# Half of the residual row joins each expert row of a routed attention layer; the last head and the first expert tiles overlap

## The chip, the cores and the metric

The kernel runs on one core of a Trainium2 chip. The metric is the device time of one execution in microseconds (us): a median of 1658.82 us over 3 runs, from 1657.81 to 1659.13.

The engines are PE (TensorE, matrix products), DVE (VectorE), ACT (ScalarE), POOL (GpSimd) and SP (SyncE, which here only starts DMA transfers). Each runs its own instruction stream; the streams meet at semaphores that one side raises and the other waits for. 16 DMA engines move data between the chip's memory (HBM) and the on-chip buffers. PE writes its sums to PSUM, eight banks of 128x512 fp32.

## The reference, cut to what matters

```
x : (2, 2048, 512) fp32;  xn = layernorm(x)
attention: 16 heads of width 32 with a latent width of 128, causal softmax
           o = concat(heads) @ Wo.T + bo
experts:   logits = xn @ gate_w + gate_b; the two best of 8 experts per token
           ffn = mean over the two of relu(xn @ expert_w[e] + expert_b[e])
result = x + o + ffn
```

There are 4096 tokens, or 32 tiles of 128. Each token has two expert rows, so 8192 expert rows are computed. They are sorted by expert and padded to PT = 72 tiles of 128 rows, so that each tile belongs to one expert.

## The kernel before

**Stages.** The first stage (to about 265 us) normalizes the rows, makes queries, keys and values, writes all of them to HBM, and works out for each token and choice its place in the sorted order (`place`) and, turned round, the token of each place (`ids`). The second stage runs 32 heads (batch x head), with PE as its busiest engine. The third computes the 72 expert tiles. The fourth projects the 32 token tiles of attention output and adds everything up.

**The head stage and its last head.** A head is NU = 20 units; each is two blocks of scores (L1274), their exponentials on ACT (L821) and, two units later, the product with the values (L1296). Units on the diagonal of the causal mask need a mask from POOL (L609) before that product; of the last chunk these are units 17 and 18 of 20. When a head's values are summed, its result goes a long way, issued by SP and spread over the next head's units: `ot_moves` (L441) copies the sums and denominators out, SP loads the denominators (L481), DVE inverts them (`invert`, L1062), SP stores them and loads them spread over the partitions (L487, L495), POOL adds two halves (`add_halves`, L612), DVE multiplies (`scale`, L1070), ACT and POOL split the product into two fp16 parts (L815, `low_part` L619), and SP keeps it in `attnT` (L502). For the last head there is no next one to spread this over. POOL also splits the expert weights into two fp16 parts during the heads (`split`, L625), one 128x512 piece per head, through the buffer `stage`, which is the memory of `x_g0`.

**The expert stage.** For tile n, POOL copies one column of `ids` to `cur_id` (L679), waits for its own copy, and gathers 128 rows of the normalized input (2 KB each, L682) into one of four buffers `x_g`; it may run four tiles ahead of PE's transposes (`gt_ps`). PE transposes tile n+1 (`turn`, L1321) and then runs the 12 matmuls of tile n (`experts`, L1339); ACT copies the transposed tile to SBUF as fp16 (L840). DVE makes the result in two operations: scale and expert bias (L1104), then relu and output bias (L1108) into one of two buffers `y_sb`. SP stores it (L530). Ahead of the loop PE waits for the last head's values to have been copied out (L1312); POOL has gone through its instructions of the last head before it gathers. SP has kept the last head (L502), loaded the projection's weights `rest` (1 MB, L524) and the residual rows of eight token tiles (`residual`, L513) before its first store.

**The last stage.** POOL waits for all stores of the expert rows (L691), then issues two gathers of 128 rows of 2 KB for each of 32 token tiles (L697), eight tiles ahead of DVE. PE makes 12 matmuls per tile (`project`, L1361) into eight PSUM banks. DVE adds in three operations (`sums`): L1118 takes the bank and the residual tile `xc` and sets the bank free (`dveE`), L1120 and L1121 add the two gathered rows. SP stores the tile (L520) and loads the residual of the tile eight further on (L514).

**Memory.** `arena2` is used by the head stage (`probs`, `q_st`, `k_st`, `v_sb`) and again by the expert stage (`xg_T`, `y_sb`, `x_ahead`, `xc`). Four `probs` buffers take its first 4096 columns, `q_st` the next 2048.

**Order.** There is no planner. The lags of the heads' steps are written out as constants in units (`ADD_LAG`, `LO_LAG`, `KEEP_LAG` and others, L315), and each engine's `heads` walks the units in one order. Loops are `Fori`; what stands in one is written once.

## Time and profile before

| what | value |
|---|---|
| median of 3 runs | 1658.82 us |
| the profiled execution itself | 1658.73 us |
| its span, first to last instruction | 1657.0 us |
| PE busy | 1516.7 us, 92% |
| DVE busy | 1149.0 us, 69% |
| ACT busy | 901.7 us, 54% |
| POOL busy | 580.0 us, 35% |
| mean granted clock of PE | 0.969 of full |

The profile is one execution. "Busy" is the time in which an engine works on an instruction; matmuls overlap one another, so PE's busy time isn't PE at its peak. In a timeline each row has a start in us from the first instruction, a length in us, the engine, the line, what is written and read, a count, and in brackets how long the engine stood idle before it and what released it. A row of stretches gives for each engine the busy us and, in brackets, the number of instructions; then the granted clock (1.00 is full), the busy share of the DMA engines and GB/s. "issue" as a releaser is time in which an engine waited for nothing that the profile shows.

### The profile page before, as it was taken

To read this page: it belongs to the slowest core of one execution; us is meant where nothing else is said; L and a number is where in the kernel's file an instruction comes from. 1 tells how busy PE (TensorE), PEld (TensorE's weight loads), DVE (VectorE), ACT (ScalarE), POOL (GpSimd) and SP (SyncE) were. 2 spreads that over 40 slices of the span, in tenths; PEclk is the share of its full clock that TensorE was granted. 3 is DMA by queue.
4 is the path that set the end of the run, shared out by engine and by line. 5 is a ranking of instruction groups with operands and counts; after the bars stand their busy time and mean duration, and the time that the engine had idled before them with its cause. 6 is when DMAs were issued, how large, how long until landed. Compare 5 with 4: busy or idle time off the path is not lost.

```text
span 1657.0 us, 44537 instructions
## 1 busy us (share of the span) xinstructions
PE 1516.7 (92%) x12544; PEld 813.2 (49%) x12545; DVE 1149.0 (69%) x2501; ACT 901.7 (54%) x1628; POOL 580.0 (35%) x780
## 2 busy tenths in 40 slices
PE   4788859999999999999999999999999599999787
PEld 2687843444444444544444444454444255555333
DVE  5677778777777777777777777777777044444356
ACT  1566644666666666666666666666667333333000
POOL 1333411344444442223223222322322333333564
PEclk9899987999999999999999999999999799999989
DMA  5488670132223222322322232232222365555687
GB/s 156 151 246 240 202 211 18 53 87 79 67 62 97 69 68 71 92 68 62 89 76 68 67 95 68 62 87 78 68 65 72 118 199 175 171 171 165 212 303 271
DMA packets 161453, 198.02 MB, mean 120 GB/s; under 512 B 45792, under 2 KB 95072, under 8 KB 161024
## 3 DMA queue, kind: packets, MB, share of 16 engines
q1 hardware_dynamic: 124224, 114.99, 23.6%
q10 hardware_dynamic: 24192, 46.72, 9.9%
q0 software_dynamic: 12992, 35.77, 7.2%
q8 instruction: 21, 0.34, 0.1%
q14 instruction: 24, 0.20, 0.0%
HBM read 109.13 MB, written 63.12 MB: 104 GB/s over the span
## 4 chain that ended last, share of the span: by engine, by line
PE 78%; DVE 10%; issue 6%; ACT 3%; DMA 1%; DVEq 1%; SPq 0%; ACTq 0%; POOL 0%; POOLq 0%
PE PS L1241 28%; PE PS L1296 28%; PE PS L1339 11%; PE PS L1361 6%; DVE pm L1053 4%; PE PS L1321 2%; ACT arena L743 1%; DVE arena L935 1%; ACT arena L763 1%; DVE stats L860 1%; DVE mx L1058 1%; PE PS L1222 1%; ACT arena L750 1%; PE PS L1187 1%; DVE mx L1057 0%
## 5 line engine op out<-in xcount | busy, mean ns | idle before, releaser
L1053 DVE TENSOR_REDUCE pm<-PS 128x1 f32<-128x512 f32 (+3 forms) x1280 | 716.0, 602 | 209.8 <-PE PS L1241 196.7
L821 ACT ACTIVATE arena<-PS 128x512 f32<-128x512 f32 (+1 forms) x1152 | 613.2, 575 | 286.3 <-PE PS L1241 267.0
L1241 PE MATMUL PS<-arena 97*64 97x512 f16 (+7 forms) x5120 | 695.6, 353 | 39.8 <-DVE pm L1053 21.1
L1296 PE MATMUL PS<-arena 128*33 128x512 f32 (+3 forms) x2560 | 634.1, 531 | 0.0
L1241 PEld LDWEIGHTS PS<-arena 97*64 97x64 f16 (+1 forms) x5120 | 330.1, 110 | 429.6 <-DVE pm L1053 142.3
L609 POOL TENSOR_SCALAR_AFFINE_SELECT arena<-arena 128x256 f32<-128x256 f32 (+1 forms) x256 | 110.6, 432 | 559.9 <-ACT arena L821 558.9
L1296 PEld LDWEIGHTS PS<-arena 128*33 128x33 f32 x2560 | 159.7, 111 | 79.0 <-POOL arena L609 0.9
L1339 PE MATMUL PS<-w_hi,arena 128*128 x576 | 172.1, 381 | 0.5 <-issue 0.5
L840 ACT ACTIVATE arena<-PS 128x1024 f16<-128x1024 f32 x72 | 73.7, 1024 | 150.8 <-PE PS L1321 148.8
L1241 PE MATMUL PS<-later,deny 128*64 128x128 f16 x1024 | 146.4, 222 | 0.0
L1104 DVE SCALAR_TENSOR_TENSOR arena<-PS,eb_bc 128x512 f32<-128x512 f32 x72 | 49.8, 692 | 128.6 <-PE PS L1339 125.2
L1361 PE MATMUL PS<-comb_hl,arena 128*128 128x512 f16 x384 | 91.7, 395 | 20.7 <-issue 20.4
L1339 PE MATMUL PS<-w_lo,arena 128*128 x288 | 109.4, 380 | 0.0
L830 ACT ACTIVATE arena<-PS 97x512 f32<-97x512 f32 x128 | 76.4, 597 | 56.3 <-PE PS L1296 38.4
L1241 PEld LDWEIGHTS PS<-later,deny 128*64 128x64 f16 x1024 | 76.0, 112 | 57.6 <-issue 25.1
L697 POOL DMA_INDIRECT w_hi<-expert_rows,place x64 | 66.6, 1040 | 49.5 <-issue 20.7
L634 POOL TENSOR_TENSOR w_hi<-x_g,ws_col 128x512 f32 (+1 forms) x32 | 33.3, 1040 | 137.7 <-DVE bv_bc L1074 137.7
L1339 PEld LDWEIGHTS PS<-w_hi,arena 128*128 128x128 f16 x576 | 53.4, 98 | 52.6 <-issue 1.7
L1361 PEld LDWEIGHTS PS<-comb_hl,arena 128*128 (+1 forms) x384 | 38.3, 100 | 74.0 <-issue 34.0
L598 POOL DMA_INDIRECT token_of_place<-token_id,place_at x64 | 62.5, 976 | 16.5 <-issue 14.4
L682 POOL DMA_INDIRECT arena<-xn_rows,cur_id x54 | 52.8, 978 | 43.8 <-POOL cur_id L679 43.0
L580 POOL TENSOR_TENSOR arena<-arena 128x512 f16<-128x512 f32 x32 | 37.2, 1163 | 81.2 <-ACT arena L737 81.2
(172 smaller groups left out, 1306.3 us busy)
## 6 DMA issues: line engine op xcount, KB each, us to landing
expert_rows<-arena SPq DMA_DIRECT2D x72, 256.0 KB, 2.1
comb_hl<-arena SPq DMA_DIRECT2D x256, 64.0 KB
arena<-q_pieces ACTq DMA_DIRECT2D x96, 128.0 KB
arena<-k_pieces ACTq DMA_DIRECT2D x96, 128.0 KB
v_rows<-arena SPq DMA_DIRECT2D x8, 1056.0 KB, 7.0
arena<-v_rows ACTq DMA_DIRECT2D x32, 264.0 KB
arena<-in_x SPq DMA_DIRECT2D x16, 512.0 KB, 5.4
xn_rows<-arena SPq DMA_DIRECT2D x16, 512.0 KB, 5.1
```

The source lines that it names most:

```text
L598: g.indirect_dma_start(out=id_dram, out_offset=bass.IndirectOffsetOnAxis(ap=place_at[:, k, i:i + 1], axis=0), in_=token_id[:, i:i + 1], in ...
L609: g.affine_select(out=both[:, :, 0:wm], in_=both[:, :, 0:wm], compare_op=ALU.is_ge, fill=nought, base=0, pattern=[[step, 2], [1, wm]], cha ...
L682: g.indirect_dma_start(out=x_g[q], out_offset=None, in_=xn_dram, in_offset=bass.IndirectOffsetOnAxis(ap=cur_id[:, q:q + 1], axis=0)).then_ ...
L697: g.indirect_dma_start(out=y_g[q][k], out_offset=None, in_=y_dram, in_offset=bass.IndirectOffsetOnAxis(ap=place[:, k, at:at + 1], axis=0)) ...
L821: a.activation(probs[kk % 4][:, a_ * CH:a_ * CH + w], PS[:, s2_bank(k, x), 0:w], ACT.Exp, scale=SCALE).then_inc(s["exp_done"], 1)
L830: a.activation(ot[q % 2][0:2 * HD + V1, :], PS[0:2 * HD + V1, 6 + q % 2, :], ACT.Copy).then_inc(s["ot_done"], 1)
L840: a.activation(xg_T[u].rearrange("p z k c -> p (z k c)"), PS[:, 4 + 2 * u:6 + 2 * u, :].rearrange("p z c -> p (z c)"), ACT.Copy).then_inc( ...
L1053: v.reduce_max(pm[:, c, r, p:p + 1], PS[:, S1_BANK[n], 0:w], AX).then_inc(s["s1_done"], 1)
L1241: last = t.matmul(PS[h:h + P // 2, bank, cols], lhsT[:, h:h + P // 2], rhs, start=start, stop=stop)
L1296: last = t.matmul(PS[rows_, 6 + c % 2, CH - wds[a]:CH], v_sb[pu % 2][:, j + a, :], probs[pk % 4][:, a * off:a * off + wds[a]], start=p_ in ...
L1339: last = t.matmul(PS[:, u, :], xg_T[u][:, z, k, :], w[:, ds(e, 1), k * E:(k + 1) * E].rearrange("p e c -> p (e c)"), start=q_ == 0, stop=q ...
L1361: last = t.matmul(PS[:, q, :], attnT[:, u * KB + k, ds(m, 1), z, at:at + P].rearrange("p o q -> p (o q)"), comb_hl[:, y, k, :], start=q_ = ...
```

## The change

Each of a token's two expert rows gets half of the token's residual row added, so that the last stage need not add it. POOL gathers the residual rows of a tile (128 rows of 2 KB of `x`) with the same list of tokens as the normalized rows, into four new buffers `xr_g`; DVE adds them with a third operation per tile. The list of tokens is copied four columns at a time. In the last stage the residual loads and one of the three additions are gone; the first of the two that are left takes the PSUM bank and the first gathered row, so the bank comes free when that row is there.

The gather of the first expert tile is issued inside the last head (unit 16 of its 20, after the last weight split), the other three right behind the head's units. PE takes the first transposes after the last exponentials, and waits for the copied-out sums only after them. The last head's steps after its denominators (`add_halves`, `scale`, `high_part`, `low_part`, `keep`) are put between the first expert tiles on each engine: on SP after six stores, and the load of `rest` behind that; on DVE after four tiles; on ACT after six. `xr_g` lies where `probs` lay; two of the buffers `x_ahead` lie where the even heads' `q_st` lay, the third where their `k_st` lay.

```diff
-        cur_id = sb("cur_id", [P, AHEAD_G], u32)
+        cur_id = sb("cur_id", [P, 2 * AHEAD_G], u32)
...
-        x_ahead = [tD(E).bitcast(f16) for _ in range(AHEAD_G - 1)]
         OUT_RING = 8
-        xc = [tD(E) for _ in range(OUT_RING)]
+        xr_g = [tD(E) for _ in range(4)]
+        x_ahead = [tD(E).bitcast(f16) for _ in range(2)]
+        tD(2 * E)
+        x_ahead += [tD(E).bitcast(f16)]
...
 # SP
-            sp.wait_ge(s["o_out"], count(16 * BH))
-            sp.dma_start(rest, comb_dram).then_inc(s["comb_in"], 16)
-            for q in range(OUT_RING):
-                residual(0, q)
...
+            for i in range(BESIDE + 1):
+                expert_rows(i)
+            keep(BH // HPB - 1, HPB - 1)
+            sp.wait_ge(s["o_out"], count(16 * BH))
+            sp.dma_start(rest, comb_dram).then_inc(s["comb_in"], 16)
+            with sp.Fori(BESIDE + 1, PT // 2) as i:
+                expert_rows(i)
+            with sp.Fori(0, NT // OUT_RING) as m:
                 for q in range(OUT_RING):
                     result(m, q)
-                    residual(m + 1, q)
...
 # POOL
+            def numbers(i, h):
+                for q in range(AHEAD_G):
+                    pool.sem_inc(s["step_at"], 1)
+                    pool.wait_ge(s[f"xr_in{q}"], (i - 1) * 16)
+                    pool.sem_inc(s["step_at"], 1)
+                now(i, h)
+            def now(i, h):
+                g.tensor_copy(cur_id[:, h * AHEAD_G:(h + 1) * AHEAD_G], ids[:, ds(i * AHEAD_G, AHEAD_G)]).then_inc(s["cur_done"], 1)
+                pool.wait_ge(s["cur_done"], count(i + 1))
+                pool.sem_inc(s["step_at"], 1)
...
+            def gather_x(i, q, h):
+                n = i * AHEAD_G + q
+                pool.wait_ge(s["y_done"], count(n - AHEAD_G + 1))
+                pool.sem_inc(s["step_at"], 1)
+                g.indirect_dma_start(out=xr_g[q], out_offset=None, in_=x_rows, ...).then_inc(s[f"xr_in{q}"], 16)
...
+                    if kk == NU + FIRST_ROWS and not more:
+                        pool.wait_ge(s["ids_in"], 16)
+                        pool.wait_ge(s["stage_free"], count(BH))
+                        now(0, 0)
+                        gather(0, 0, 0)
...
+            for q in range(1, AHEAD_G):
+                gather(0, q, 0)
+            pool.wait_ge(s["pv_done"], count(NU * BH))
+            for q in range(AHEAD_G - X_BEHIND):
+                gather_x(0, q, 0)
+            add_halves(BH - 1, 1)
+            def both_rows(i, h):
                 for q in range(AHEAD_G):
+                    gather(i, q, h)
+                    if q < X_BEHIND:
+                        gather_x(i - 1, (q - X_BEHIND) % AHEAD_G, 1 - h)
+                    else:
+                        gather_x(i, q - X_BEHIND, h)
+            now(1, 1)
+            both_rows(1, 1)
+            low_part(BH - 1)
+            with pool.Fori(1, PT // (2 * AHEAD_G)) as i:
+                for h in range(2):
+                    numbers(i * 2 + h, h)
+                    both_rows(i * 2 + h, h)
...
 # ACT
+            for n in range(2 * (BESIDE + 1)):
+                turned(n, n % 2)
+            high_part(BH - 1)
...
 # DVE, expert tile
                     v.scalar_tensor_tensor(out=y_sb[u], in0=y_sb[u], scalar=0.0, in1=bo_bc[:],
-                                           op0=ALU.max, op1=ALU.add).then_inc(s["y_done"], 1)
+                                           op0=ALU.max, op1=ALU.add).then_inc(s["relu_done"], 1)
+                    dve.wait_ge(s["relu_done"], count(n + 1))
+                    dve.wait_ge(s[f"xr_in{q}"], (i4 + 1) * 16)
+                    v.scalar_tensor_tensor(out=y_sb[u], in0=xr_g[q], scalar=1.0 / TOP, in1=y_sb[u],
+                                           op0=ALU.mult, op1=ALU.add).then_inc(s["y_done"], 1)
+            rows(0)
+            scale(BH - 1, 1)
+            with dve.Fori(1, PT // AHEAD_G) as i:
+                rows(i)
...
 # DVE, last stage
-                lnk(v.scalar_tensor_tensor(out=acc[q], in0=PS[:, q, :], scalar=1.0 / WS, in1=xc[q], op0=ALU.mult, op1=ALU.add))
                 dve.wait_ge(s[f"yg_in{q}"], (m + 1) * (16 * TOP))
-                lnk(v.tensor_tensor(acc[q], acc[q], y_g[q][0], ALU.add))
+                lnk(v.scalar_tensor_tensor(out=acc[q], in0=PS[:, q, :], scalar=1.0 / WS, in1=y_g[q][0], op0=ALU.mult, op1=ALU.add))
                 v.tensor_tensor(acc[q], acc[q], y_g[q][1], ALU.add).then_inc(s["acc_done"], 1)
...
 # PE
-            pe.wait_ge(s["ot_done"], count(NC * BH))
...
+            pe.wait_ge(s["exp_done"], count(NX * BH))
             turn(0, 0, 0)
+            pe.wait_ge(s["ot_done"], count(NC * BH))
```

## Rows read from the trace of the kernel before

**Rows 1.** The stretches of the end: the gap, the expert loop, the last stage.
```profile
core 0: us, PE busy (x) PEld busy (x) DVE busy (x) ACT busy (x) POOL busy (x), PEclk, DMA share, GB/s
1299.20:1317.60 18.40, 0.00 (x0) 0.00 (x0) 1.12 (x3) 1.13 (x2) 4.95 (x7) 0.58 0.24 54
1317.60:1328.00 10.40, 9.22 (x56) 4.99 (x57) 1.48 (x3) 3.07 (x3) 5.65 (x9) 0.76 1.00 384
1328.00:1540.00 212.00, 211.88 (x1388) 112.51 (x1385) 96.80 (x140) 70.64 (x69) 75.67 (x130) 1.00 0.54 170
1540.00:1564.00 24.00, 22.61 (x104) 10.21 (x105) 12.00 (x18) 0.00 (x0) 14.90 (x15) 1.00 0.69 226
1564.00:1584.00 20.00, 5.81 (x11) 1.13 (x11) 2.32 (x4) 0.00 (x0) 13.34 (x14) 0.61 0.89 281
1584.00:1657.00 73.00, 63.28 (x269) 26.98 (x268) 51.78 (x77) 0.00 (x0) 38.32 (x36) 0.94 0.81 288
```

**Rows 2.** Chain of waits by time (start us, us, what), last head to experts.
```profile
1296.90 2.18 PE PS L1296 x9
1301.05 1.79 DMA denominators<-arena
...
1307.00 2.98 DMA bv_bc<-inverses
...
1315.76 3.40 DMA arena<-xn_rows,cur_id
...
1320.56 3.72 PE PS L1339 x12
...
1328.20 2.59 PE PS L1339 x12
```

**Rows 3.** Timeline of POOL, end of the last head and first gathers.
```profile
1295.05 1.16 POOL L623 TENSOR_TENSOR o_st<-bv_bc,o_st 128x512 f16<-128x512 f32 x1
1296.16 0.77 POOL L609 TENSOR_SCALAR_AFFINE_SELECT arena<-arena 128x256 f32<-128x256 f32 x2
1303.01 1.26 POOL L617 TENSOR_TENSOR comb_hl<-comb_hl 128x512 f32<-128x512 f32 x1 [6.08 <-issue]
...
1314.74 0.19 POOL L679 COPY cur_id<-ids 128x1 uint32<-128x1 uint32 x1
1315.76 0.98 POOL L682 DMA_INDIRECT arena<-xn_rows,cur_id  x1 [0.82 <-POOL cur_id L679]
```

**Rows 4.** Timeline of DVE, one expert tile.
```profile
1455.44 0.69 DVE L1104 SCALAR_TENSOR_TENSOR arena<-PS,eb_bc 128x512 f32<-128x512 f32 x1 [1.52 <-PE PS L1339]
1456.17 0.69 DVE L1108 SCALAR_TENSOR_TENSOR arena<-arena,bo_bc 128x512 f32<-128x512 f32 x1
```

**Rows 5.** Timeline of POOL beside it, a copy of the token list.
```profile
1456.45 0.46 POOL L679 COPY cur_id<-ids 128x1 uint32 x1
```

**Rows 6.** DMA queues, 1350 to 1530 us: packets, MB, share of 16 engines.
```profile
q0 software_dynamic: 4705, 15.41, 31.2%
q1 hardware_dynamic: 8489, 15.46, 23.5%
```

**Rows 7.** DMA queues, 1545 to 1657 us.
```profile
q0 software_dynamic: 5120, 16.78, 45.2%
q1 hardware_dynamic: 8064, 14.68, 36.7%
```

**Rows 8.** Groups by line, 1545 to 1657 us (busy us, mean ns).
```profile
L697 POOL DMA_INDIRECT w_hi<-expert_rows,place x64 | 66.6, 1040 | 49.5 <-issue 20.7 <-DMA expert_rows<-arena 20.1 <-DVE w_lo L1121 8.7
```

**Rows 9.** Timeline of POOL, first gather of the last stage.
```profile
1544.83 0.95 POOL L697 DMA_INDIRECT w_hi<-expert_rows,place  x1 [20.15 <-DMA expert_rows<-arena]
```

**Rows 10.** Timeline of DVE: last expert row, one stall, last sum.
```profile
1540.75 0.69 DVE L1108 SCALAR_TENSOR_TENSOR arena<-arena,bo_bc 128x512 f32<-128x512 f32 x1
...
1583.03 0.69 DVE L1118 SCALAR_TENSOR_TENSOR w_lo<-PS,arena 128x512 f32<-128x512 f32 x1 [16.91 <-issue]
...
1653.70 0.69 DVE L1121 TENSOR_TENSOR w_lo<-w_lo,w_hi 128x512 f32<-128x512 f32 x1
```

More of the change, by code:

```diff
@@ L497, in heads, with keep @@
                     hk = kk - KEEP_LAG
-                    if 0 <= hk and hk % NU == HEAD_END:
-                        w, hd = hk // NU, j * HPB + hk // NU
+                    if 0 <= hk and hk % NU == HEAD_END and (hk // NU < HPB - 1 or more):
+                        keep(j, hk // NU)
+            def keep(j, w):
+                        hd = j * HPB + w
                         sp.wait_ge(s["o_lo_done"], count(hd + 1))
@@ L521, in result, with expert_rows @@
                              ).then_inc(s[f"out_done{q}"], 16)
[L523 to L527 removed]
+            def expert_rows(i):
                 for u in range(2):
@@ L1086, in heads @@
                     hk = kk - MUL_LAG
-                    if 0 <= hk and hk % NU == HEAD_END:
+                    if 0 <= hk and hk % NU == HEAD_END and (hk // NU < 1 or more):
                         scale(it * 2 + hk // NU, hk // NU)
```

77 lines of the change are left out of this document (34 added, 43 removed).

## Prediction

> **What bounds the kernel now.** I read the page first: PE is busy 92% of the span, and the 40 slices show it full except near the beginning, in one slice after the heads and at the end. The change touches nothing before the last head, so I then took the stretches from there [rows 1], where each row gives busy time by engine, the granted clock, and DMA share. Three things are to be seen. From 1299.2 to 1317.6 us PE does nothing and its clock falls (0.58 of full, mean). From 1328 to 1540 PE is full at clock 1.00: 1388 matmuls at 20 per tile make 69.4 tiles in 212 us, 3.05 us each; DMA is 0.54 busy. After 1540 PE has 384 matmuls at 22.61/104 = 0.217 us, 83.5 us of work, but the end comes 117 us later. In 1564 to 1584 it makes 11 matmuls in 20 us while POOL goes on issuing gathers and DMA is 0.89 busy, and DVE stands 16.9 us with "issue" as its releaser [rows 10].
>
> The chain of waits [rows 2] says what the gap is: the last head's sums end at 1299.08, then denominators go out, come back, are inverted and spread, POOL ends the head, and only then the first gathers run. The expert stage is PE; the last stage is transfers, gather issue and the stall.
>
> **The gap.** Removed: the last head's tail and the wait for it. Added on the path: the first gather stands on POOL ahead of two masks. POOL ends `low_part` at 1296.21 [rows 3]; copy 0.19, gap 0.82, gather 0.98 put the first mask at 1298.2 in place of 1296.16. PE's last nine to twelve value products wait for those masks, so its end moves by 2.0 us, from 1299.1 to 1301.1. The first gather starts at 1297.2 and lands 3.4 us later, going by the 3.40 of the chain's gather [rows 2], at 1300.6: in time. `turn(0)` takes some 0.6 us. Gather 1 follows the masks (two in 0.77 us, end 1299.0) at 1299.2 and lands at 1302.6; `turn(1)` then lets tile 0 start at 1303.1. Gathers 2 and 3 and two residual gathers follow at 1.28 each (0.98 and a gap of 0.30: in the last stage 20.7 us of "issue" stand ahead of 60 gathers [rows 8], 0.34 each with a few long ones among them).
> Tile 2 then starts at 1303.1 + 2 x 3.05 = 1309.2; before, at 1328.2 [rows 2]. That is 19.0 us. Before, tiles 0 and 1 took 7.64 us instead of 6.1 because the clock was down (0.76 in 1317.6 to 1328, rows 1); after, PE is idle only in gaps of 2 us or less, but it works little from 1301 to 1303, so I charge 1.0 of that 1.5 again. Next, POOL is just in time: after residual gathers at 1303.0 and 1304.3 come `add_halves` (1.26, rows 3) to 1306.6, the copy, and gather 4 at 1307.6, landing 1311.0 against a need at the end of tile 2, 1311.8. Four pairs later (1317.6) POOL waits for the last head: tile 3 ends 1315.3, three DVE operations 2.2, `scale` 0.7, ACT 0.6 and `low_part` 1.16 make 1320.1; gather 8 starts 1321.1 and lands 1324.5, needed at 1324.4. The projection's 1 MB load also moves into this loop. I charge 1.5 us for both. Gap: -19.0 + 1.0 + 1.5 = -16.5, bounds -19 and -13.
>
> **The expert loop.** Per tile it adds one DVE operation, 0.69 and 0.03 [rows 4]: 2.2 us of 3.05, hidden under PE; the y store's buffer is then free 0.7 us later, with some 1 us left before its next use. It adds 256 KB of gather. DMA-engine time per transfer [rows 6]: 60 tiles in 180 us, so some 59 gathers (80 packets each) in 31.2% of 180 us are 0.95 us each, and 59 stores 0.72. In the last stage a gather costs 45.2% of 112 / 64 = 0.79 [rows 7]. Two gathers and a store are 2.3 to 2.6 us of 3.05, a share of 0.76 to 0.86. Right behind the gap DMA ran at 1.00 and 384 GB/s with PE not starved [rows 1], so this is hidden.
> POOL is the tight one. Per four tiles: eight gathers at 0.98 + 0.30 are 10.2, and the one copy with its wait 0.7 more than a gap: 10.9, against 12.2 for PE. To that comes the block by DVE. The copy at 1456.45 took 0.46 instead of 0.18 us, and ended with DVE's L1108, which had started at 1456.17 [rows 4, 5]. The mean gather of the last stage, beside DVE's additions, is 1.04, not 0.95 [rows 8, 9]. With two such operations in a row (1.42 us) longer than a gather's pitch, at least one gather per tile starts in them and waits: nothing at best, 0.69 at worst, half an operation (0.35) on the mean. 10.9 + 4 x 0.35 = 12.3, 0.1 over PE, for 17 rounds: +2. Bounds: 10.9, so 0; and 10.9 + 2.8 = 13.7, so +26.
> The Trainium skill (SBUF — State Buffer, Who interferes with whom) states that a DVE instruction with two SBUF inputs contends with a GpSimd instruction that reads SBUF, and that the second to issue blocks until the first ends. By that rule the added operation (`xr_g` and `y_sb`) doubles the blocked time; the trace's 0.46 us agrees. The sum would be what I have, or the worse rival below if the two engines fall into step.
>
> **The last stage.** Removed: 24 residual loads (eight were loaded early) at 36.7% of 112 / 56 = 0.73 us of DMA time each, 17.6 us in all, and 32 DVE operations. DMA-engine time asked for while POOL runs ahead falls from (2 x 0.79 + 2 x 0.73) / 2.52 = 1.21 to 0.92, so no backlog grows. I take the 20 us stall to come with that backlog, since it falls where POOL issues 14 gathers in a row [rows 1]; that is inference. What sets the end is then POOL: DVE's last expert row is at 1541.44 [rows 10], 0.7 later by the third operation; first gather 3.39 after it [rows 9]; 64 gathers at 1.02 + 0.30 are 84.2 (1.02 lies between 0.95 and 1.04, as DVE makes two additions per 2.6 us and one of them has two SBUF inputs); landing 2.4 after the last; two additions 1.4; store to the end 2.6 (1657.0 less 1654.39). Sum 94.7, against 115.6 before: -20.9. PE's 83.5 fits below. PSUM banks now wait for gathers, but gathers lead by about 10 us. For throttling and queues I charge 1.9: -19. Bounds: a pitch of 1.26 and nothing charged, -25; and the removed DMA work wholly hidden, with the stall kept, -4.
>
> **Sum.** -16.5 + 2 - 19 = -33.5 against the profiled execution's 1658.7 (span 1657.0 and 1.7 around it; the median of the runs is 0.1 higher): 1625.2. I predict 1625.
>
> **Rivals.**
> (A) POOL becomes the bound of the expert loop. After one gather per tile blocked 0.5 us, gather and residual gather take 1.28 + 1.28 + 0.5 = 3.06, PE's own period, so the two keep in step, and the 0.7 of each copy is never made up. 0.7 more x 17 is +12, less 1 of lead: +11 over my +2: 1636. For: rows 4 and 5. Against: an offset list is read only at a gather's start, and phases shift. 0.2.
> (B) The stall stays in the last stage: then some 15 of the 19 us there are not gained, 1640. For: DMA share would still be near 0.88 with two gathers and a store, as in the stalled 20 us (0.89). Against: in 1584 to 1657 it is 0.81 and PE mostly runs. 0.15.
> (C) Slower than before: the stall comes into the expert loop, whose DMA share rises from 0.54 to about 0.8. Each 20 us of it costs PE 17.6 (11 matmuls of 0.217 in 20 us). It decides from two such stretches, 35 us against my 33.5. A quarter of the loop, 54 us, costs 48: 1673. For: POOL would issue gathers nearly without a pause in both places. Against: 1.00 share at 1317.6 to 1328 without it. 0.07.
> (D) Better: no block, no charge, gathers at 1.26: 1658.7 - 19 - 25 = 1615. 0.08.
> Also possible is that the first gather isn't in time in the last head, so that only the tail goes; its price is within the gap's bounds.
>
> **Chances and range.** My forecast has 0.5 and its own range 1618 to 1633. With A, B and D the range 1614 to 1644 leaves out C and A with B together. Measurement tells 0.2%, 3.3 us, from no change. Faster 0.91, same 0.03 (A and B with a short stall in the loop), slower 0.06.
>
> **What would show it.** PE's first expert matmul near 1303 with the clock hardly down; two masks near 1298.2; the last head's steps behind tiles 3 to 6. In the loop a period of 3.05 to 3.1, POOL busy near 90%, DMA share 0.75 to 0.86, gathers of 1.0 to 1.5 us; a period of 3.2 or more with PE waiting for `xn_rows` gathers is A. In the last stage 64 gathers in about 85 us and no PE pause with "issue"; a stretch of single matmuls is B. The prediction is wrong if PE waits for POOL or for masks by more than 3 us at the start, or if the last stage stays above 105 us.

## The result, and the profile after

The changed kernel takes **1678.4 us** (median of 4 runs, 1676.0 to 1682.6) against 1659.0 for the kernel before beside it (4 runs): ratio **1.0119, 95% interval 1.0103 to 1.0136**. Forecast were 1625 and "faster"; it is slower by 19.4 us. The profiled execution has a span of 1677.5 us, 20.5 more than before.

Three stretches make the 20.5. The limits are the starts of PE's first and last expert matmul and the end of the span, from the matmul records; each figure is rounded by itself.

| stretch | before | after | measured | forecast |
|---|---|---|---|---|
| first expert matmul | 1320.6 | 1303.2 | -17.4 | -17.5 at tile 0 |
| expert matmuls, first to last | 218.9 | 251.9 | +33.0 | +3 with the start's charges |
| last expert matmul to the end | 117.5 | 122.4 | +5.0 | -19 |

The windows of the changed kernel by stage (columns as in rows 1) answer to those of [rows 1]:
```profile
1299.20:1317.60 18.40, 14.94 (x102) 7.44 (x98) 6.38 (x11) 5.70 (x6) 12.86 (x15) 1.00 0.68 204
1317.60:1328.00 10.40, 8.91 (x52) 4.31 (x52) 8.91 (x13) 3.59 (x4) 5.84 (x6) 1.00 0.52 159
1330.00:1540.00 210.00, 188.09 (x1202) 97.76 (x1201) 123.33 (x178) 60.12 (x61) 129.02 (x138) 0.99 0.75 234
1578.00:1602.00 24.00, 5.77 (x14) 1.32 (x13) 2.77 (x4) 0.00 (x0) 15.53 (x16) 0.62 0.77 242
1602.00:1677.00 75.00, 65.76 (x276) 27.71 (x274) 34.89 (x52) 0.00 (x0) 35.15 (x36) 0.93 0.67 217
```
The gap is filled: PE works 14.9 of 18.4 us where it stood, at clock 1.00. In the expert loop PE is no longer full: 188.1 of 210 us, though POOL is busy only 0.61 and the DMA engines 0.75. The last stage again has a stretch with hardly a matmul (14 in 24 us), at a DMA share of 0.77 instead of 0.89.

The chain of waits in the loop (start, length, what) shows the form of the loss, which the chain before has nowhere in its expert loop:
```profile
1352.35 0.55 PE PS L1375 x8
1352.90 0.02 issue
1352.92 0.04 ACTq L886
1352.96 0.04 issue
1353.00 0.05 ACT arena L887
1353.05 6.50 another core or an unknown queue
1359.55 0.02 issue
```
and POOL's timeline of the same time (start, length, line; in brackets its idle time before):
```profile
1350.85 0.97 POOL L663 DMA_INDIRECT x_g<-xn_rows,cur_id  x1 [0.97 <-PE PS L1375]
1352.12 1.02 POOL L672 DMA_INDIRECT arena<-in_x,cur_id  x1 [0.30 <-issue]
1353.44 0.94 POOL L663 DMA_INDIRECT arena<-xn_rows,cur_id  x1 [0.30 <-issue]
1354.69 1.02 POOL L672 DMA_INDIRECT arena<-in_x,cur_id  x1 [0.30 <-issue]
1356.01 0.95 POOL L663 DMA_INDIRECT arena<-xn_rows,cur_id  x1 [0.30 <-issue]
1357.26 0.95 POOL L672 DMA_INDIRECT arena<-in_x,cur_id  x1 [0.30 <-issue]
1360.35 0.94 POOL L663 DMA_INDIRECT arena<-xn_rows,cur_id  x1 [2.14 <-PE PS L1375]
```
ACT's copy of a turned tile (L887) waits for semaphores that PE raises, with its turn (L1375) and with the matmuls of an earlier tile. The next turn ends at 1355.8, the earlier matmuls before it, and nothing but their semaphores is missing; yet the copy starts at 1359.65:
```profile
1359.65 1.94 ACT L887 ACTIVATE arena<-PS 128x1024 f16<-128x1024 f32 x2 [5.63 <-remote]
```
POOL issues six gathers in a row without a wait in that time and stops at 1358.2; the semaphore arrives 1.3 us later, and POOL's own wait for PE ends with it. In the waits of 1330 to 1550 this is the line with "remote", a releaser that the profile can't name:
```profile
ACT arena L887 <- PE PS L1375: 97.9, 34, 7.9
ACT arena L887 <- remote: 50.3, 12, 5.6
```
(us in total, times, longest.) Pauses are counted here and below from the start of one expert matmul to the start of the next; where the turn of a tile stands between them the normal step is 0.67 us. Those of the last stage are counted between its matmuls, each less the normal step of 0.22 us. PE's matmul records have 20 pauses over 1.2 us in the loop, from 1398 on mostly one of about 2.4 us every 14 us, which is every four tiles.

In the last stage PE itself hardly goes on: its matmuls come one by one, while POOL issues gathers at its full pitch and PE's idle time has no releaser:
```profile
1593.47 0.58 PE L1417 MATMUL PS<-comb_hl,arena 128*128 128x512 f16 x1 [2.91 <-issue]
1594.89 0.58 PE L1417 MATMUL PS<-comb_hl,arena 128*128 128x512 f16 x1 [0.83 <-issue]
```

### The profile page after: what moved, and what is told of

Its sections match the earlier page's. It is cut to its first block, busy times and chain, and to the rows that moved or that the text cites. A ratio compares the mean times of both kernels' runs of the same rounds, so it can differ in the third digit from the quotient of the medians.

```text
span 1677.5 us, 44548 instructions
## 1 busy us (share of the span) xinstructions
PE 1523.4 (91%) x12544; PEld 811.2 (48%) x12545; DVE 1178.8 (70%) x2541; ACT 901.1 (54%) x1628; POOL 643.6 (38%) x798
## 4 chain that ended last, share of the span: by engine, by line
PE 73%; DVE 10%; issue 7%; ACT 4%; another core or an unknown queue 3%; DMA 2%; DVEq 1%; POOL 0%; SPq 0%; ACTq 0%; POOLq 0%
PE PS L1297 27%; PE PS L1352 27%; PE PS L1393 8%; PE PS L1417 6%; DVE pm L1103 4%; PE PS L1375 2%; ACT arena L887 1%; DVE arena L985 1%; PE PS L1278 1%; DVE stats L910 1%; DVE mx L1108 1%; ACT arena L787 1%; ACT arena L807 1%; PE PS L1282 1%
## 5 line engine op out<-in xcount | busy, mean ns | idle before, releaser
L613 POOL TENSOR_SCALAR_AFFINE_SELECT arena<-arena 128x256 f32<-128x256 f32 (+1 forms) x256 | 110.6, 432 | 559.7 <-ACT arena L868 558.6
L887 ACT ACTIVATE arena<-PS 128x1024 f16<-128x1024 f32 x72 | 72.2, 1022 | 177.5 <-PE PS L1375 106.4
L1417 PE MATMUL PS<-comb_hl,arena 128*128 128x512 f16 x384 | 92.3, 397 | 25.6 <-issue 25.6
L672 POOL DMA_INDIRECT arena<-in_x,cur_id x72 | 74.5, 1035 | 40.5 <-DVE arena L1162 17.8
L741 POOL DMA_INDIRECT w_hi<-expert_rows,place x64 | 62.0, 969 | 44.5 <-issue 17.6
L1176 DVE SCALAR_TENSOR_TENSOR w_lo<-PS,w_hi 128x512 f32<-128x512 f32 x32 | 22.0, 689 | 71.8 <-remote 25.5
```

The lines of the kernel that those rows point to most:

```text
L613: g.affine_select(out=both[:, :, 0:wm], in_=both[:, :, 0:wm], compare_op=ALU.is_ge, fill=nought, base=0, pattern=[[step, 2], [1, wm]], cha ...
L672: g.indirect_dma_start(out=xr_g[q], out_offset=None, in_=x_rows, in_offset=bass.IndirectOffsetOnAxis(ap=cur_id[:, h * AHEAD_G + q:h * AHEA ...
L741: g.indirect_dma_start(out=y_g[q][k], out_offset=None, in_=y_dram, in_offset=bass.IndirectOffsetOnAxis(ap=place[:, k, at:at + 1], axis=0)) ...
L887: a.activation(xg_T[u].rearrange("p z k c -> p (z k c)"), PS[:, 4 + 2 * u:6 + 2 * u, :].rearrange("p z c -> p (z c)"), ACT.Copy).then_inc( ...
L1417: last = t.matmul(PS[:, q, :], attnT[:, u * KB + k, ds(m, 1), z, at:at + P].rearrange("p o q -> p (o q)"), comb_hl[:, y, k, :], start=q_ = ...
```

## The experiments

Three theories were told apart. **G**: gathers that POOL issues one behind another, for some 6 us and more, hold up the other engines. **B**: the added bytes or transfers do it. **L**: VectorE's operations with two SBUF inputs slow POOL's gathers, and POOL is the bound. The kernel before took 1658.6 us on the chip of e1 to e4, 1663.8 on that of e5 to e8, 1659.8 on that of e9 to e12, **1637.9** on that of e13 to e15, 1662.4 beside e16 and e17 (the chip of e5 again), 1663.0 on that of e18. e2, e3, e4, e6, e7, e9, e10, e13 and e18 are single executions; the trace of each is what counts, and differences of a few us between them are not read.

**e1, the overlap alone** (residual added in the last stage as before):
```diff
-  v.scalar_tensor_tensor(out=y_sb[u], in0=xr_g[q], scalar=1.0 / TOP, ...)   # and all gather_x
+  lnk(v.tensor_tensor(acc[q], acc[q], y_g[q][0], ALU.add))                   # last stage as before
```


> The overlap of the last head with the first expert tiles alone; residual rows are loaded and added in the last stage as before, and the list of tokens is copied four columns at a time. Every theory takes the loss to lie in the added gathers and not in the overlap: 1640 to 1646 us (13 to 19 us under the kernel before), with the expert loop at 3.05 us a tile and the last stage as before, 117 us, with its 20 us stall. If the overlap itself costs (masks late, clock down, POOL just in time), it comes out at 1650 or more.


Measured: 1656.6 (10 runs), ratio 0.9992 (0.9983 to 1.0002): not the 1640 to 1646 expected, and no gain beyond noise. Experts 1302.2 to 1532.6, 230.4 us: the whole gap is gained (18.4) and 11.5 given back at the loop's start, in pauses at 1310.9, 1323.8 and 1337.0 of 1.2, 3.1 and 6.7 us. The last is VectorE's 9.9 us wait for a y store: SyncE had queued the 1 MB load and eight residual loads (1329.1 to 1333.4), behind a wait, ahead of it. No pause after that. So the 14 us loop pattern comes of the residual's part, and the overlap loses most of its own gain at the loop's start.

**e2, residual rows by plain loads; e3, residual gathers of a quarter row:**
```diff
-  gather_x(...)                                                  # e2: POOL
+  sp.dma_start(xr_g[q], x_rows[q * P:(q + 1) * P, :])            # e2: SP, same bytes
-  x_rows = x.rearrange("b s d -> (b s) d")                       # e3
+  x_rows = x.rearrange("b s (f d) -> (b s f) d", f=4)            # 512 B per row, into [:, 0:P]
```


> The changed kernel with each residual gather replaced by a plain load of 128 rows (256 KB) that SP issues into the same buffer; always the same 512 rows of x, so the residual isn't each token's own. Bytes, DVE's third operation and the last stage stay. Theory G (it is POOL's gathers, issued one behind another for 10 us and more, that hold up the other engines): the loop goes back to 3.05 us a tile, the pauses of 2 to 5 us are gone, and the time falls by some 20 us to 1655 to 1660. Theory B (it is the bytes, 0.76 DMA share instead of 0.54): the pauses stay, 1675 to 1680. Theory L (DVE's two-input operations block POOL's gathers, POOL becomes the bound): POOL issues only one gather per tile, so as G, 1655 to 1660.

> The changed kernel with residual gathers of 512 bytes per row instead of 2 KB (a quarter of the residual, of other rows); the same number of gathers, of DVE operations and of waits. Theory G: no change within 8 us, 1670 to 1680. Theory B: the loop goes back to near 3.05 us a tile, 1655 to 1660. Theory L: no change, POOL still issues 144 gathers.


Measured: e2 1657.9, loop 233.7; e3 1674.3, loop 251.1. The stretch 1380 to 1500, clear of the start, one row for the changed kernel, then e2, then e3 (columns as in rows 1):
```profile
1380.00:1500.00 120.00, 108.95 (x706) 57.22 (x705) 74.13 (x107) 33.94 (x34) 72.86 (x78) 1.00 0.74 229
```
```profile
1380.00:1500.00 120.00, 120.00 (x789) 63.90 (x788) 82.20 (x120) 40.87 (x40) 48.87 (x50) 1.00 0.83 260
```
```profile
1380.00:1500.00 120.00, 109.42 (x709) 57.44 (x707) 73.30 (x105) 34.67 (x35) 71.23 (x79) 1.00 0.55 170
```
With all bytes and VectorE's third operation but half the gathers, PE is full at a DMA share of 0.83. With a quarter of the changed kernel's traffic gone (170 GB/s for 229) and all gathers kept, it loses the same 11 us as the changed kernel. **B falls.**

**e4 and e8, at most 3 tiles ahead in the last stage,** in the changed kernel and in the kernel before:
```diff
-  if n >= OUT_RING: pool.wait_ge(s["acc_done"], count(n - OUT_RING + 1))
+  if n >= 3:        pool.wait_ge(s["acc_done"], count(n - 3 + 1))
```


> The changed kernel with POOL's gathers of the last stage held at three token tiles ahead of DVE instead of eight. Theory G: the stall of the last stage (24 us, from the sixteenth of a row of gathers on) comes from POOL issuing gathers without a pause, and a limit of six gathers puts pauses in: the stage takes 95 to 105 us in place of 122, 1655 to 1663. Theory B: bytes per us stay nearly the same, the stall stays, within 5 us of 1678. A code-loading stall at the first pass of the loop's body: stays too.

> The kernel before with POOL's gathers of the last stage held at three tiles ahead of DVE instead of eight. Theory G: the 20 us stall shrinks as it did in the changed kernel (stage 122 to 111 us): 1646 to 1654. If the residual loads on SP make the difference there: 1657 to 1662.


Measured: e4 1666.3, last stage 111.3 (122.4 without the limit), pauses of its projection 6.4 us (25.6); the stage was expected at 95 to 105. e8 1652.9 (4 runs), **ratio 0.9937 (0.9916 to 0.9958)**, last stage 114.7 (117.5), pauses 1.2 (22.0). In e8 the window that had 11 matmuls [rows 1] reads
```profile
1564.00:1584.00 20.00, 17.15 (x59) 6.00 (x59) 11.29 (x17) 0.00 (x0) 12.42 (x12) 0.83 0.92 316
```
The stall goes while the DMA share rises to 0.92, with no transfer taken away. It was never a backlog; it came of POOL running ahead. Side by side it is worth 0.63%, 10.5 us, in e8; the profiled execution shows only 2.7 of them in the last stage, but against a profile from another chip. Of the 20.8 us of pauses most aren't won in that trace: with the limit VectorE waits for gathers to land instead (26.1 us at L1120, 9.4 before).

**e5, e1 with SyncE's order mended:**
```diff
-  sp.wait_ge(s["o_out"], count(16 * BH)); sp.dma_start(rest, comb_dram)
-  for q in range(OUT_RING): residual(0, q)
+  for i in range(BESIDE + 1, BESIDE + 1 + OUT_RING):
+      expert_rows(i); residual(0, i - BESIDE - 1)
+  sp.dma_start(rest, comb_dram)
```


> The overlap alone, as in the first experiment, with SP's order mended: after the last head is kept, SP goes on storing expert rows at once, with one residual load behind every second store, and loads the projection's weights after those. Theory: the overlap's gain was eaten by SP (3 MB of loads ahead of the store that DVE waited for, 6.7 us of PE at 1337) and by two smaller pauses. Then that pause goes and the time is 1648 to 1652. If what ate it is the row of gathers at the start, the pauses at 1311 and 1324 stay and grow, 1655 to 1658.


Measured: 1649.4 (4 runs), **ratio 0.9915 (0.9893 to 0.9937)**. Loop 222.2, 3.3 over before. So of e1's 11.5 us, 8 go with SyncE's queue, by one trace each from two chips.

**e6, every second residual tile gathered:**


> The changed kernel with the residual of every second tile gathered and of the others loaded plainly by SP (fixed rows of x, so the residual isn't each token's own). POOL has 1.5 gathers per tile of 3.05 us in place of 2. Theory G in the form that a pause of POOL of some length clears what its gathers hold up: POOL issues for some 2.0 us of each 3.05 and pauses in each tile, so the loop runs as with plain loads, 1656 to 1660. If each gather costs the others a fixed time: half of the 16.5 us between the plain and the narrow variant, 1665 to 1667.


Measured: 1664.0 (expected 1656 to 1660; kernel before 1663.8), loop 235.7 with four pauses up to 1349.5 and none after. In its trace the six gathers per four tiles come one to three at a time, POOL waiting for PE's turn ahead of most of them. Half the added gathers bring not half of the pattern but none of it.

**e7 and e10, POOL as busy, without the residual gathers** (plain loads, and in their place on POOL one operation):
```diff
+  g.tensor_tensor(scrap_half, bo_bc[:], eb_bc[:, 0, :], ALU.subtract)   # e7, 128x512, two inputs
+  g.memset(scrap, 0.0)                                                  # e10, 128x1024
```


> The variant with plain loads (the residual isn't each token's own), with a subtraction of 128x512 on POOL (1.04 to 1.16 us each, no use made of the result) where the residual gather had stood, under the same wait. POOL is as busy as in the changed kernel. Theory G (the issue of gathers itself): no pauses, as with plain loads, 1656 to 1661. Theory L and rival A (POOL has too much to do, and its gathers of normalized rows come late): as the changed kernel, 1674 to 1680.

> The kernel with plain residual loads (x_plain), with a memset of 128x1024 on GpSimd (estimate 1.0 us, from 519 ns for 128x512 in the kernel before) where the changed kernel issues each residual gather. The residual rows are not those of the token, so the output is not the reference's. GpSimd is as busy as in the changed kernel, but with an operation that reads nothing and issues no DMA. Theory G, in its form that it is the issue of gathers and not GpSimd's being busy: no regular pauses of 2.4 us; loop 232 to 238 us, time 1656 to 1662. If being busy without a pause is what counts, the pauses come as in the changed kernel: loop 246 to 252, time 1672 to 1678. The run with a two-input operation there (1676.4) could not tell these apart, because its own operation and VectorE's slowed each other.


Measured: e7 1676.4, loop 246.2; e10 1663.4, loop 236.8. e10's row for 1380 to 1500:
```profile
1380.00:1500.00 120.00, 120.00 (x789) 63.95 (x788) 82.25 (x120) 40.83 (x40) 83.07 (x90) 1.00 0.83 257
```
POOL is busier than in the changed kernel (83.1 against 72.9) and PE is full. Being busy is not it. e7 (expected at 1656 to 1661 by G) lost time in another way: VectorE's L1175, two SBUF inputs, took 957 ns in the mean where its counterpart L1158 takes 702 beside gathers:
```profile
L1175 DVE SCALAR_TENSOR_TENSOR arena<-arena,bo_bc 128x512 f32<-128x512 f32 x38 | 36.4, 957 | 1.3
```
and the waits there name y stores and PE, not "remote". The two engines' two-input operations hold each other up; it says nothing on gathers. The Trainium skill (SBUF — State Buffer, Who interferes with whom) states that a VectorE instruction with two SBUF inputs contends with a GpSimd instruction that reads SBUF, and not with one that only writes it. Here the traces agree: 0.26 us more per operation beside e7's subtractions, and 692 ns, nothing more, beside e10's memsets. e7 was a badly chosen test of G; e10 replaced it.

**e9 and e12, 3 tiles ahead in the expert loop** (e12: in the last stage too):
```diff
-  pool.wait_ge(s["gt_ps"], count(n - AHEAD_G + 1))      # and y_done for the residual rows
+  pool.wait_ge(s["gt_ps"], count(n - 2))
```


> The changed kernel with one thing altered in the expert loop: GpSimd may issue the gather of a tile's token rows and of its residual rows only 3 tiles ahead of their use (it waits for the turn and the rows of the tile three before, where it waited for the fourth before). The same gathers, bytes, VectorE operations and stores; the output is the reference's. Theory G (an unbroken run of gathers on GpSimd holds up the other engines' semaphores): each gather now follows an event of TensorE or VectorE, one pair in 3.3 us, so GpSimd pauses for 0.4 us or so after each and never issues 8 in a row; the pauses of 2.4 us every 13.9 us go, the loop from first to last expert matmul takes 232 to 238 us (changed kernel: 251.9; with plain loads: 233.7), and the time is 1658 to 1664. Theory L (VectorE's two-input operations slow GpSimd's gathers until GpSimd is the bound) and theory B (bytes): GpSimd has the same work and less freedom, so the loop takes 252 us or more and the time is 1678 to 1684.

> The changed kernel with GpSimd 3 tiles ahead both in the expert loop and in the last stage; the output is the reference's. Theory G: the loop's gain of e9 (15 to 20 us) and the last stage's of e4 (11 us by span to span) add, time 1644 to 1652, so the whole change would be worth 7 to 14 us over the kernel before, with what is left of the loop's pauses at its start. Theories L and B: only the last stage's gain, 1665 to 1672.


Measured: e9 1679.8, loop 251.7; e12 1667.3 (8 runs), ratio 1.0044 (1.0032 to 1.0057), loop 252.1, last stage 114.3. Not a microsecond in the loop: the expectations by G (loop 232 to 238, e12 at 1644 to 1652) failed. Its trace shows why the edit did not do what it was for. The hole around the copy of the numbers (1450.05 to 1452.69, POOL idle 1.4 and 1.0) makes POOL late, the waits are fulfilled before it comes to them, and it issues six in a row (1452.69 to 1459.93) as before; ACT's semaphore is late again, to 1461.54. So e9 shows only that a limit which isn't reached doesn't space gathers.

**e11, the best version** (e5 and 3 tiles ahead in the last stage):


> The candidate for the best version: first gathers within the last head and the order of SyncE's transfers mended as in overlap_sp, the residual added in the last stage as before, and GpSimd at most 3 tiles ahead with the gathers of the last stage. The output is the reference's. If the two gains are independent they add: 0.9915 (overlap with SyncE's order) times 0.9937 (three ahead in the kernel before) is 0.985, or 1635 us for a kernel before of 1659. If the last stage is bound by another thing once the first gain is taken (its transfers), the sum falls short: 1643 to 1647.


Measured: **1638.3 (4 runs), ratio 0.9869 (0.9853 to 0.9885)**. Loop 222.9, last stage 110.6. The two gains add nearly in full (0.9915 x 0.9937 = 0.9852). The window that answers to the stall:
```profile
1550.00:1570.00 20.00, 17.38 (x77) 7.23 (x76) 12.35 (x20) 0.00 (x0) 12.52 (x13) 1.00 0.96 329
```

**e13 and e18, bursts.** e5's kernel (its first eight residual loads two at a time) with extra gathers ahead of some groups of four tiles, the same program on two chips:
```diff
+  if i == 5:  2 x extra(q)          # extra: g.indirect_dma_start(out=xc[q], ..., ids[:, q:q+1])
+  if i == 7:  4 x extra(q)
+  if i == 10: 8 x extra(q)
+  if i == 12: 16 x g.memset(xc[q], 0.0)
+  if i == 15: 5 x (extra(q); g.memset(xc[5 + q % 3], 0.0))
```


> A dose and response within one run. Base: the overlap alone with SyncE's order mended (loop 222.2 us, no pause after 1333), with the first eight residual rows loaded within the first 13 tiles. GpSimd then puts extra work before a group's four gathers: 2 extra gathers of 128 residual rows ahead of tiles 20 to 23, 4 ahead of tiles 28 to 31, 8 ahead of tiles 40 to 43, 16 memsets of 128x512 (about 8.3 us) ahead of tiles 48 to 51, and 5 gathers with a memset behind each ahead of tiles 60 to 63. The extra gathers put other tokens' rows in the first eight residual buffers, so the output is not the reference's. Theory G (an unbroken run of gathers delays the other engines): no pause of TensorE near the 2, none or one near the 4, pauses of 2 us and more near the 8 (a run of 8 and the 4 regular behind them), none near the memsets and none or a short one near the 5 spaced ones, though GpSimd is busy as long there. Theory L (GpSimd only becomes late as the bound): the pauses at the 8, at the 16 memsets and at the 5 spaced ones are alike, since all keep GpSimd from its own gathers for 8 to 10 us, and where TensorE pauses it waits for a gather's landing, not for a semaphore of ScalarE or TensorE that comes late.

> The kernel of e13, with its bursts of 2, 4 and 8 extra gathers, 16 memsets and 5 spaced gathers on GpSimd (other tokens' rows in the first eight residual buffers, so the output is not the reference's), run again for a chip on which the kernel before takes some 1660 us. On the chip of e13 (kernel before 1638) even thirteen gathers in a row (1417.14 to 1434.48) held up no semaphore: TensorE paused once, 4.3 us from 1429.3, and waited for a gather's landing. Theory G with the chip's part in it: on a slow chip TensorE pauses 2 to 4 us within some 7 to 10 gathers of a burst's start, with its semaphores coming late at ScalarE, not at the memsets, and the last stage has its 22 to 26 us of pauses again; loop 235 to 245 us. Theory L: as in e13, one pause behind the 8 and TensorE waits for a landing.


Measured: e13 1636.3 (before: 1637.9), e18 1663.8 (before: 1663.0). PE's pauses over 1.2 us (counted as above) in the loop after its start:

| extra work | e18 | e13 |
|---|---|---|
| 2 gathers | none | none |
| 4 gathers | 2.6 at 1384.7 | none |
| 8 gathers | 8.2 at 1423.1 | 4.3 at 1429.3 |
| 16 memsets, 7.5 us | 1.2 at 1462.8 | none |
| 5 gathers, each with a memset behind it | 2.0 at 1499.8 | 1.8 at 1495.6 |

The 8 in e18, chain and POOL's timeline, lines left out between:
```profile
1418.01 12.07 another core or an unknown queue
1430.08 0.02 issue
```
```profile
1417.05 0.95 POOL L724 DMA_INDIRECT arena<-in_x,ids  x1 [0.30 <-issue]
1418.30 0.95 POOL L724 DMA_INDIRECT arena<-in_x,ids  x1 [0.30 <-issue]
...
1425.82 0.95 POOL L724 DMA_INDIRECT arena<-in_x,ids  x1 [0.30 <-issue]
1426.77 0.19 POOL L661 COPY cur_id<-ids 128x4 uint32<-128x4 uint32 x1
1427.87 0.97 POOL L670 DMA_INDIRECT x_g<-xn_rows,cur_id  x1 [0.91 <-issue]
1430.88 0.94 POOL L670 DMA_INDIRECT arena<-xn_rows,cur_id  x1 [2.05 <-remote]
```
PE ran out at 1423.9, 6.9 us after the burst began; what it lacked was ACT's copy of the turned tile, not a gather. A turn that ended at 1420.9 was seen by ACT at 1430.18, 1.3 us after POOL stopped (1428.84); POOL's own wait was "remote" too. In e13 the same burst (from 1417.14) kept on to 1427.3 with four regular gathers behind it, and the chain goes through POOL and then a landing, a wait for data that isn't there yet:
```profile
1428.41 3.84 DMA x_g<-xn_rows,cur_id
1432.25 0.05 issue
1432.30 0.62 PE PS L1405 x8
```
So G holds on e18's chip, as cause and not only as company: 4 and 8 gathers in a row bring late semaphores, 7.5 us of memsets do not. And it **does not hold on e13's chip**: thirteen gathers from 1417.14 to 1434.48 with only two copies of the list between them, no late semaphore, and no stall in the last stage (98.7 us; 121.9 in e18).

**e14 and e17, the copy of the numbers ahead of a group's last residual gather; e15, that with e5's SyncE order and e4's limit; e16, the changed kernel again:**
```diff
   for q in range(AHEAD_G):
       gather(i, q, h)
+      if q == AHEAD_G - 1: numbers(i + 1, 1 - h)     # the copy; waited for at the group's start
```


> The changed kernel with one thing moved: GpSimd copies the next four tiles' numbers (L654) ahead of the last residual gather of a group, not behind it, so that the copy's completion (0.97 us of waiting) and the gathers that read the other half have another gather beside them. The output is the reference's. In e9 GpSimd's hole around the copy was 1.7 to 2.7 us in four tiles (gather issued at 1450.05, next at 1452.69), which with eight gathers of 1.26 us makes 12.4 of the 13.2 us that TensorE needs. If being late behind that hole is what makes GpSimd issue six gathers without a wait, it is now early, waits for an event before most gathers, and theory G gives a loop of 233 to 240 us and 1660 to 1666. Theory L (GpSimd is the bound) gives the hole back alone: 1.5 us in four tiles, up to 27 us, but not below GpSimd's own 10.4 in 13.2, so the same sign; what tells the two apart is e13 and whether the late semaphores go with it. If neither, the loop stays at 252 us.

> The whole change with the three mends: the copy of the numbers moved ahead (e14), SyncE's 1 MB load ten tiles later and without the wait in front of it, and GpSimd at most 3 tiles ahead in the last stage. The output is the reference's. If e14 mends the loop: 233 less some 6 us of the start, last stage 111, together 1640 to 1650, no better than the overlap alone with the same two mends (1638.26). If it does not: 1658 to 1664.

> The changed kernel itself, unaltered, beside the kernel before on the same chip. The kernel before took 1658 to 1664 us on the chips of the earlier runs and 1638 us on the chip of e13 to e15, where its last stage cannot have had the pauses of 22 us (the traces of e13 to e15 have none there, and their last stages take 98 to 105 us where the same code took 119 to 123). If the pauses belong to some chips and not to others, there are two outcomes: on a chip where the kernel before takes some 1659 us, the changed one takes 1676 to 1682 again (ratio 1.010 to 1.014), with pauses every four tiles; on one where it takes some 1638 us, it takes 1630 to 1640, with a loop of about 235 us and a last stage of about 98.

> The changed kernel with the copy of the numbers ahead of the group's last residual gather, as in e14, beside the changed kernel on one chip. On the chip of e14 it took 1636.6 with a loop of 232.8 us; whether the earlier copy or the chip made that loop short is open, since the changed kernel was not run there. If the earlier copy takes the pauses away (theory G by way of GpSimd being early), its loop is 233 to 240 us where the changed kernel's is 250 or more, and it is 12 to 17 us faster than the changed kernel. If the chip did it, the two are within 3 us of each other on either kind of chip.


Measured: e14 1636.6 (10 runs), ratio 0.9985 (0.9973 to 0.9998); e15 1643.3 (10 runs), 1.0030 (1.0019 to 1.0041); e16 1681.8 (4 runs), 1.0112 (1.0084 to 1.0141); e17 1677.3 (4 runs), 1.0093 (1.0072 to 1.0115). e14 and e17 are one program. Their row for 1380 to 1500 and their longest kind of ACT wait there, on e17's chip and then on e14's:
```profile
1380.00:1500.00 120.00, 111.87 (x724) 58.55 (x722) 74.76 (x109) 34.81 (x36) 74.68 (x80) 1.00 0.76 234
ACT arena L896 <- remote: 51.0, 12, 5.0
```
```profile
1380.00:1500.00 120.00, 118.40 (x777) 62.72 (x776) 80.43 (x117) 39.35 (x39) 83.25 (x89) 1.00 0.82 251
ACT arena L896 <- PE PS L1384: 81.4, 39, 2.6
```
The chip made e14's loop short (232.8; 249.7 in e17), not the copy: e17 is 4.5 us under the changed kernel beside it, and their two intervals overlap. (e16 came as expected for such a chip; e14's 1636.6 lies far under the 1660 to 1666 expected.) On e14's chip the last stage is 98.5 us:
```profile
1564.00:1605.00 41.00, 41.00 (x192) 18.57 (x191) 22.23 (x32) 0.00 (x0) 31.25 (x33) 1.00 0.93 304
```
PE full, POOL far ahead, DMA at 0.93, no stall. The kernel before is 21 to 26 us faster on that chip than on the others, about the 22 us of its stall; it has no trace from that chip. So L doesn't hold either: with 89 POOL operations in 120 us, PE is 0.99 busy. e15's limit costs there (last stage 104.7), where nothing needs it. Its other mend, SyncE's 1 MB load later (by 16 tiles in its edit, not by ten), gives nothing there (loop 235.4): the load now goes out at 1383, and a 4.4 us wait of VectorE for a y store stands behind it, with a pause of PE of 4.2 us at 1390.

**Whose semaphores are late.** The packed traces hold the moment of each recorded increment. In the table an increment is late when it comes over 0.3 us after the end of the last instruction ahead of it that raises that semaphore. With some records missing this is a lower bound. The ends of matmuls are modelled, but where nothing stalls PE's increments follow them by 0.01 to 0.02 us, or 0.1 us once in e10. Stretch 1380 to 1500:

| run | PE's increments recorded | late | of these at most |
|---|---|---|---|
| before | 77 | 0 | |
| changed kernel | 52 | 26 | 3.3 us |
| e2, plain loads | 78 | 0 | |
| e3, narrow gathers | 51 | 31 | 3.4 us |
| e6, every second tile | 66 | 6 | 0.9 us |
| e7 and e10, POOL busy | 142 | 0 | |
| e9 | 52 | 27 | 3.9 us |
| e17 | 61 | 28 | 3.4 us |
| e14, the program of e17 on the chip without the stall | 78 | 0 | |

Of the increments that VectorE, ScalarE and GpSimd's own copies raise, 114 recorded in the changed kernel, not one comes over 0.02 us after its instruction, in this stretch or in those of the other runs. So it is TensorE that is held up: what it raises comes late to the others, and in the last stage its own matmuls trickle. ACT and POOL, which seemed to be held up too, were waiting for it.

Two more causes are to be asked for. Loading of code is not it in the loop: from 1336.3 to 1543.5 the changed kernel's trace has no packet of an instruction queue, and the pattern runs all the while. The recording of the trace isn't excluded. In the heads (300 to 1290 us, the same work in every run) 167 to 187 of some 6200 semaphore records are missing on each chip with the stall, and 1 to 4 on the one without. So the chips differ in how their records get out as well; no execution on record is known to be without the recording, and whether it has a part in the stall isn't shown.

## Why the prediction was wrong, step by step

**The gap: right.** The masks ran at 1297.45 (forecast 1298.2), gather 1 at 1298.39 (1299.2), the first expert matmul came at 1303.2 (1303.1). PE waited 1.9 us for the masks (2.0). The 1.0 us charged for the clock wasn't needed: it stayed at 1.00.

**The start of the loop: mis-sized.** 1.5 us were charged. The pauses up to 1345 sum to 9.4 us over the normal step. The forecast had gather 8 start at 1321.1 and land just in time; the chain has
```profile
1323.17 0.65 POOL cur_id L654
1324.02 0.54 issue
1324.66 0.11 issue
1324.78 3.99 DMA x_g<-xn_rows,cur_id
1328.82 0.62 PE PS L1375 x8
```
so it landed 4.3 us later than forecast. Two things were left out. One is the stall itself, which is there from the start: POOL issues eight gathers from 1307.9 to 1318.7, the turn that ends at 1312.9 is seen by ACT at 1315.1, and the late tile makes `scale`, `low_part` and so gather 8 late; the pause at 1336.5 is a late semaphore as well. The other is e1's finding: SyncE's queue stands ahead of y stores. The text said that the load "moves into this loop" and priced it with a lump; between e1 and e5, with eight residual loads beside it, the queue's order goes with 8 us. On the chip without the stall (e14) the start's pauses are as long, 8.9 us, and there VectorE waits for y stores (13.4 us up to 1346). How the changed kernel's 9.4 divide between the two isn't shown.

**The expert loop: the step that failed.** The term was +2, from the block of POOL's gathers by VectorE, with POOL as the tightest resource and nothing for a long row of gathers; the loop took +33. The block is real but smaller than the 0.35 us per tile of the sum: from 1380 to 1500 the 26 gathers that start within a two-input VectorE operation take 1.13 us in the mean, up to 1.45, the other 43 take 0.95 and none over 0.97. That is 0.14 us per tile. POOL was not the bound: busy 0.61 where the text looked for 0.9, it waited for PE. What came is rival C, the slower one, which had 0.07: the stall of the last stage appeared in the expert loop. Even C had the form wrong. It priced long stretches of 20 us; what came are pauses of 2.4 us in every four tiles, since POOL's run ends each time at its next wait. PE's loss from 1380 to 1500 is 11.05 us of 120 (rows of e2 and the changed kernel), 9.2%; over some 200 us that is 18. e2, which has the loop's start and not the pattern, takes 14.8 us more than the kernel before, and 18 and 15 make the 33.

**The last stage: failed for the same reason.** The text took the stall "to come with that backlog" and called it inference. Taking 24 loads and 32 operations away lowered the DMA share from 0.89 to 0.77 in the stalled stretch and left the stall at 25.6 us. The row that could have told was there: POOL went on at its pitch of 1.26 us while DVE stood with "issue" for 16.9 us [rows 10], where these views name the transfer if its landing ends the wait. And the counter-example I leaned on, DMA at 1.00 from 1317.6 to 1328 without a stall [rows 1], was one against bandwidth, which I read as comfort. POOL's gathers there, and in the whole expert loop before, stand at least 2.0 us apart, since a copy and a gap of 0.82 precede each [rows 3]. The change makes one copy for eight gathers and so takes away that spacing too, which the text counted only as time saved.

**The chip.** The forecast's 98.5 us for the last stage (117.5 - 19) is what e14's last stage takes, 98.5. That is no success of the forecast: on that chip the kernel before is 21 to 26 us faster than on the others, without the change.

**Still open.** What path gathers and TensorE's semaphores share; whether the recording of the trace has a part in it; why one chip of the five that can be told apart is free of it; whether the changed kernel itself is faster than before there (only e14's form ran there, ratio 0.9985, and the one part of it that differs is worth 4.5 us by the medians elsewhere, with intervals that overlap).

## What to carry to other kernels

Where the chip has the stall, count the longest unbroken run of gathers that an edit lets GpSimd issue, not only its busy share: let it wait for a consumer every two or three, and do not let it run further ahead than the landing needs; that alone gave 0.6% to the kernel before. On the chip without it the limit cost: the last stage took 104.7 us in e15, 98.5 in e14. A stall in which several engines stand with "issue" or "remote" while one of them issues DMAs at full pitch is to be tested by limiting that engine before it is explained by bandwidth. A transfer that moves into a loop is priced by what stands behind it on its queue (8 us here for a load off every engine's path), and a gain of 1% should be measured on more than one chip: here the kernel before differs by 1.3 to 1.6% between chips.

## What the runs showed of the hardware

- On four of five chips (that of the first result isn't known to be another), while GpSimd issues gathers at a pitch of 1.25 us without a wait, the semaphores that TensorE raises come up to 9 us late (1420.9 to 1430.1 in e18), and 0.6 to 1.3 us after GpSimd stops (1385.4 to 1386.05 and 1428.84 to 1430.1 in e18, 1358.2 to 1359.55 in the changed kernel). Those that the other engines raise come within 0.02 us. Four extra gathers are enough, two are not; 128x512 memsets for 7.5 us do nothing of it, and gathers with a memset between them hardly.
- Rows of 512 B and of 2 KB do it alike (e3), so it goes by gathers or by rows (128 in each), which no run tells apart, and not by bytes.
- On the fifth there is nothing of it, with the same program and thirteen gathers in 17 us; the kernel before is 1637.9 us there against 1658.6 to 1663.8.
- A gather that starts while VectorE runs an operation with two SBUF inputs takes 1.13 us in the mean (up to 1.45), one that doesn't 0.95 (changed kernel, 69 gathers from 1380 to 1500).
